# Self-attention on one core: residual on ScalarE, products and output bias on VectorE, reciprocal roots by a power on GpSimd

## The reference, cut to what matters

```python
# layer 0 (its attention part ends in this projection)
attn = softmax(logits) @ v            # 8 heads of 8
x = x + concat([conv_out, attn @ attn_w + attn_b])
# layer 1, self-attention, 1024 tokens of 256
u = (t - mean(t)) / sqrt(var(t) + 1e-5)
Q, K, V = u @ W_q, u @ W_k, u @ W_v   # 128 wide
out = softmax(Q @ K.T / sqrt(128)) @ V
t = t + out @ W_o + b_o + u           # u is added as well
v2 = (t - mean(t)) / sqrt(var(t) + 1e-5)   # input of the experts
```

## Time and profile before

| | |
|---|---|
| median of 3 runs | 2439.54 us (2436.12 to 2440.03) |
| profiled execution, its own time | 2439.41 us |
| its span | 2437.7 us |
| TensorE busy | 2185.6 us, 90% |
| VectorE busy | 1344.4 us, 55% |
| ScalarE busy | 1214.6 us, 50% |
| GpSimd busy | 330.2 us, 14% |
| mean granted TensorE clock | 0.929 |

### The profile page before, as it was taken

One profiled execution on the slowest core, in us unless ns is written; L12 is line 12 of the kernel. 1 busy time (PEld: TensorE's weight loads), 2 busy tenths in 40 slices (PEclk: granted clock), 3 DMA queues, 4 the chain that ended last, 5 costly groups with the idle time before them and its releaser, 6 DMA issues. The chain is left out here.

```text
span 2437.7 us, 32845 instructions
## 1 busy us (share of the span) xinstructions
PE 2185.6 (90%) x10534; PEld 1512.9 (62%) x10534; DVE 1344.4 (55%) x2054; ACT 1214.6 (50%) x2160; POOL 330.2 (14%) x274
## 2 busy tenths in 40 slices
PE   4999999947999999999999974988888893999997
PEld 3777888846445454444454422777777772888886
...
DMA packets 150472, 268.33 MB, mean 110 GB/s; under 512 B 31808, under 2 KB 94016, under 8 KB 146240
## 3 DMA queue, kind: packets, MB, share of 16 engines
...
...
...
## 5 line engine op out<-in xcount | busy, mean ns | idle before, releaser
L652 DVE TENSOR_REDUCE a_nmax<-a_sm 128x1 f32<-128x1024 f32 x512 | 604.0, 1220 | 209.9 <-PE a_sm L672 209.6
L908 ACT ACTIVATE p_shared<-a_st 128x512 f32<-128x512 f32 x1024 | 556.6, 596 | 252.4 <-PE a_st L933 250.9
L948 PE MATMUL a_pv<-p_shared,a_va 128*32 128x512 f32 x2048 | 275.1, 610 | 0.9 <-ACT p_shared L908 0.9
L933 PE MATMUL a_st<-a_qf,a_kf 121*128 121x512 f32 x704 | 257.5, 444 | 18.8 <-issue 8.6
L933 PEld LDWEIGHTS a_st<-a_qf,a_kf 121*128 121x128 f32 x704 | 121.0, 192 | 220.1 <-ACT p_shared L908 198.7
L672 PE MATMUL a_sm<-a_kf,a_qf 120*128 120x512 f32 x704 | 218.3, 429 | 40.8 <-DMA a_kf<-kq_d 25.0
L1823 PE MATMUL x_h_ps<-x_v_hi,x_w 128*128 128x512 f32 x512 | 181.0, 395 | 24.9 <-DVE x_v_lo L1764 24.9
L672 PEld LDWEIGHTS a_sm<-a_kf,a_qf 120*128 120x128 f32 x704 | 136.4, 204 | 78.8 <-issue 25.8
L1837 PE MATMUL x_y_ps<-x_h_hi,x_w 128*128 128x512 f32 x512 | 178.0, 389 | 0.0
L1774 DVE SCALAR_TENSOR_TENSOR x_h_lo<-x_hid,x_wts,x_h_hi 128x512 fp32r<-128x512 f32 x128 | 96.1, 751 | 138.3 <-ACT x_h_hi L1745 138.3
L1741 ACT ACTIVATE x_hid<-x_h_ps,x_b 128x512 f32<-128x512 f32 x128 | 88.4, 691 | 131.0 <-PE x_h_ps L1823 126.0
...
## 6 DMA issues: line engine op xcount, KB each, us to landing
...
```

The costliest lines, as they stand in the source:

```text
L652: nc.vector.tensor_reduce(nmax[:, h, t:t + 1], sm[k % 2][:], axis=AX.X, op=ALU.max, negate=True).then_inc(sm_read, 1)
L908: nc.scalar.activation(probs[:, t % 2, h, half * HALF:(half + 1) * HALF], st[half][:], ACT.Exp).then_inc(exp_done, 1)
L933: nc.tensor.matmul(st[half][:], kf[j][0:ROW_M + 1, h, t * P:(t + 1) * P], qf[j][0:ROW_M + 1, h, 2 * t // TT, half * HALF:(half + 1) * HALF ...
L948: m = nc.tensor.matmul(pv[32 * h:32 * h + 32, cols], va[j][:, t, h, :], probs[:, t % 2, h, cols], start=t == 0, stop=t == TT - 1, skip_gro ...
```

## The change

- `res` is a new step. On ScalarE it makes `xb` times (1 + rstd) plus `shift` in place, with four activations (t + u in one pass). VectorE makes `grow` = rstd + 1 in `apply`, and in `res` adds `bo` over 128x1024. `res 0` stands at the end of slot 5, `res 1` in slot 7, both at the end of `FRONT`.
- `norm` is a new step: the product of `att` and `rsb` on VectorE, in slots 0 and 1, at the head of `FRONT`. `proj 0` moves from slot 0 to slot 1.
- The reciprocal roots are one power (exponent -0.5) on GpSimd; the logarithms and exponentials on ScalarE and both uses of `newton` on VectorE go.
- ScalarE's `apply` no longer waits for `res_ready`.

```diff
         BETWEEN = [
-            [("out", 2, -1), ("probs", 7, -1), ("proj", 0, 1), ("vt", 1, 0), ("turn", 0, -1)],
-            [("probs", 0, 0), ("half", 3, -1), ("turn", 1, -1), ("mix", 0, 1)],
+            [("out", 2, -1), ("probs", 7, -1), ("norm", 0, 1), ("vt", 1, 0), ("turn", 0, -1)],
+            [("probs", 0, 0), ("proj", 0, 1), ("half", 3, -1), ("turn", 1, -1), ("norm", 1, 1), ("mix", 0, 1)],
...
-            [("turn", 3, -1), ("k", 0, 1), ("half", 1, 0), ("vt", 0, 1), ("apply", 1, 1)],
+            [("turn", 3, -1), ("k", 0, 1), ("half", 1, 0), ("vt", 0, 1), ("apply", 1, 1), ("res", 0, 1)],
...
-            [("q", 1, 1), ("probs", 6, 0), ("vvar", 0, 0), ("half", 2, 0), ("k", 1, 1), ("vapply", 0, 0), ("v", 1, 1), ("values", 2, 0)]]
+            [("q", 1, 1), ("probs", 6, 0), ("vvar", 0, 0), ("half", 2, 0), ("k", 1, 1), ("res", 1, 1), ("vapply", 0, 0), ("v", 1, 1),
+             ("values", 2, 0)]]
...
-                        if what == "proj":
...
-                            nc.gpsimd.tensor_tensor(att[k][:], att[k][:], rsb[k][:], ALU.mult).then_inc(norm_ready, 1)
-                        if what == "apply":
...
-                            nc.gpsimd.tensor_tensor(x1, x1, u[:], ALU.add)
...
-                            nc.gpsimd.tensor_tensor(x1, x1, bo_all, ALU.add).then_inc(res_ready, 1)
+                        if what == "var":
+                            pool.wait_ge(var_ready, n * 2 + k + 1)
+                            nc.gpsimd.tensor_tensor(rstd[:, k], var[:, k], power[:], ALU.pow).then_inc(rstd_ready, 1)
+                        if what == "vvar":
+                            pool.wait_ge(vart_ready, n * 2 + k + 1)
+                            nc.gpsimd.tensor_tensor(rstdt[:, k], vart[:, k], power[:], ALU.pow).then_inc(rstdt_ready, 1)
...
-                            act.wait_ge(res_ready, n * 2 + k + 1)
...
+                        elif what == "res":
+
+                            for i in range(QT):
+                                last = nc.scalar.activation(xb[s][:, k * QT + i, :], xb[s][:, k * QT + i, :], ACT.Identity,
+                                                            bias=shift[:, k, i:i + 1], scale=grow[:, k, i:i + 1])
+                            last.then_inc(grown_ready, 1)
...
+                            nc.vector.tensor_scalar(grow[:, k], rstd[:, k], 1.0, None, ALU.add)
+                            nc.vector.scalar_tensor_tensor(shift[:, k], mv[:, :, 0], -1.0, rstd[:, k], ALU.mult, ALU.mult).then_inc(shift_ready, 1)
+                        elif what == "res":
+                            dve.wait_ge(grown_ready, n * 2 + k + 1)
+                            x1 = xb[s][:, k * QT:(k + 1) * QT, :]
+                            nc.vector.tensor_tensor(x1, x1, bo_all, ALU.add).then_inc(res_ready, 1)
+                        elif what == "norm":
+
+                            dve.wait_ge(att_loaded[k], n * (16 * (1 + GROUPS)) + 16 * (1 + GROUPS))
+                            nc.vector.tensor_tensor(att[k][:], att[k][:], rsb[k][:], ALU.mult).then_inc(norm_ready, 1)
...
-                            newton(nc, dve, rstdt[:, k], vart[:, k], tmpt[:, k])
```

More of the change, by code:

```diff
@@ L999, in self_attention @@
         st6, mv = sb("b_st6", [P, QT, 6]), sb("b_mv", [P, QT, 2])
-        var, rstd, tmp, shift = (sb(f"b_{n}", [P, 2, QT]) for n in ("var", "rstd", "tmp", "shift"))
+        var, rstd, grow, shift = (sb(f"b_{n}", [P, 2, QT]) for n in ("var", "rstd", "grow", "shift"))
+        power = sb("b_power", [P, QT])
         u = sb("b_u", [P, QT, C])
@@ L1016, in self_attention @@
         st6t, mvt = sb("b_st6t", [P, QT, 6]), sb("b_mvt", [P, QT, 2])
-        vart, rstdt, tmpt = (sb(f"b_{n}", [P, 2, QT]) for n in ("vart", "rstdt", "tmpt"))
+        vart, rstdt = (sb(f"b_{n}", [P, 2, QT]) for n in ("vart", "rstdt"))
         v2 = sb("b_v2", [P, QT, C])
@@ L1031, in self_attention @@
         c_read = sem("b_c_read")
-        var_ready, rstd_ready, shift_ready, u_ready, res_ready = (sem(f"b_{n}_s") for n in ("var", "rstd", "shift", "u", "res"))
+        var_ready, rstd_ready, shift_ready, u_ready, grown_ready, res_ready = (
+            sem(f"b_{n}_s") for n in ("var", "rstd", "shift", "u", "grown", "res"))
         uhi_ready, bhi_ready = sem("b_uhi_s"), sem("b_bhi_s")
@@ L1063, in self_attention @@
              ("probs", 4, 0), ("turn", 2, -1), ("var", 1, 1), ("q", 0, 1), ("v", 0, 1)],
-            [("turn", 3, -1), ("k", 0, 1), ("half", 1, 0), ("vt", 0, 1), ("apply", 1, 1)],
+            [("turn", 3, -1), ("k", 0, 1), ("half", 1, 0), ("vt", 0, 1), ("apply", 1, 1), ("res", 0, 1)],
             [("out", 0, 0), ("values", 1, 0), ("ut", 2, 1), ("probs", 5, 0), ("out", 1, 0), ("ut", 3, 1)],
-            [("q", 1, 1), ("probs", 6, 0), ("vvar", 0, 0), ("half", 2, 0), ("k", 1, 1), ("vapply", 0, 0), ("v", 1, 1), ("values", 2, 0)]]
-        FRONT = [("proj", 0), ("proj", 1), ("mix", 0), ("mix", 1), ("mix", 2), ("var", 0), ("mix", 3), ("apply", 0), ("var", 1),
-                 ("ut", 0), ("ut", 1), ("apply", 1), ("sums", 0), ("q", 0), ("k", 0), ("v", 0), ("vt", 0), ("ut", 2), ("ut", 3), ("q", 1), ("k", 1), ("v", 1)]
+            [("q", 1, 1), ("probs", 6, 0), ("vvar", 0, 0), ("half", 2, 0), ("k", 1, 1), ("res", 1, 1), ("vapply", 0, 0), ("v", 1, 1),
+             ("values", 2, 0)]]
+        FRONT = [("norm", 0), ("norm", 1), ("proj", 0), ("proj", 1), ("mix", 0), ("mix", 1), ("mix", 2), ("var", 0), ("mix", 3), ("apply", 0), ("var", 1),
+                 ("ut", 0), ("ut", 1), ("apply", 1), ("sums", 0), ("q", 0), ("k", 0), ("v", 0), ("vt", 0), ("ut", 2), ("ut", 3), ("q", 1), ("k", 1), ("v", 1),
+                 ("res", 0), ("res", 1)]
         def period(b, s, before, after):
@@ L1205, in _ @@
             def _(pool):
+                nc.gpsimd.memset(power[:], -0.5)
                 nc.gpsimd.memset(wp[:], 0.0).then_inc(consts, 1)
@@ L1228, in _ @@
             def _(act):
-                def rsqrt(out, in_):
-                    nc.scalar.activation(out, in_, ACT.Ln)
-                    act.drain()
-                    return nc.scalar.activation(out, out, ACT.Exp, scale=-0.5)
                 def run(steps):
@@ L1251, in run @@
                                                  ).then_inc(b_read, 1)
-                        elif what == "var":
-                            act.wait_ge(var_ready, n * 2 + k + 1)
-                            rsqrt(rstd[:, k], var[:, k]).then_inc(rstd_ready, 1)
-                        elif what == "vvar":
-                            act.wait_ge(vart_ready, n * 2 + k + 1)
-                            rsqrt(rstdt[:, k], vart[:, k]).then_inc(rstdt_ready, 1)
                         elif what == "apply":
                             act.wait_ge(shift_ready, n * 2 + k + 1)
-                            act.wait_ge(res_ready, n * 2 + k + 1)
                             if k:
@@ L1318, in spread @@
                     nc.vector.tensor_scalar(v, m[:, :, 1], 1e-5, None, ALU.add).then_inc(ready, 1)
-                def scales(m, r, v, tm, sh, ready):
-                    newton(nc, dve, r, v, tm)
-                    nc.vector.scalar_tensor_tensor(sh, m[:, :, 0], -1.0, r, ALU.mult, ALU.mult).then_inc(ready, 1)
+                bo_all = bo[:].rearrange("p (a c) -> p a c", a=1).to_broadcast([P, QT, C])
                 def run(steps):
@@ L1366, in run @@
                             if k % 2 == 0:
-                                dve.wait_ge(res_ready, n * 2 + k // 2 + 2)
+                                dve.wait_ge(res_ready, n * 2 + k // 2 + 1)
                                 dve.wait_ge(t_stored[k // 2], n * 16 + 16)
@@ L1372, in run @@
                             last.then_inc(c_read, 1)
-                dve.sem_inc(res_ready, 1)
                 dve.wait_ge(sums_loaded[0], 16)
```

7 lines of the change are left out of this document (removed).

## The result

The changed kernel takes **2449.22 us** (median of 6 runs, 2446.65 to 2452.63) against 2439.61 us for the kernel before (6 runs, 2436.12 to 2440.37) on the same chip: +9.6 us, a ratio of 1.004 with a 95% interval of 1.0027 to 1.0052. The profiled execution took 2448.74 us with a span of 2447.0 and a mean granted clock of 0.937 (before 2439.41, 2437.7 and 0.929). So the change costs time, as forecast, but a third of the +27.1 us that the prediction added up. The steps that went as predicted and those that didn't are best seen apart, so the rows come first.

What follows compares the result with a forecast made beforehand. The prediction took TensorE, working in order almost without gaps, as busiest, with VectorE held by GpSimd in slot 4. Terms -31.2 + 26.6 + 12.2 + 5.6 + 7.9 + 6.5 - 0.5 = +27.1 gave 2466.5 us, range 2437 to 2482.

Steps and rivals of the forecast that it cites:

- the clock that stays up: Rival: the clock doesn't fall in the new TensorE gaps, so the change costs +9.4, 2449 us; chance 0.20.
- slot 4, images 1 to 6: Scores 4 to 5: without GpSimd's large operations holding VectorE, 5.2 us won per image, -31.2 us.
- slots 5 and 6, seven images, without clock: `res 0` delays the exponential of scores 6, and `out 1` waits: 3.8 us an image, +26.6 us.
- clock behind that gap: After TensorE's gap of some 3.6 us before `out 1` the clock falls in seven images, +12.2 us.
- slots 7, 0, 1: `res 1` delays the next scores 0 and `turn 0`, the projection moves to slot 1: 7 x 0.8, +5.6 us.
- two loop-backs: VectorE's 3.08 us of issue stays, TensorE's gap becomes 3.8 us and drops the clock: +7.9 us.
- front and image 0's slots 0, 1: Both `res` before the first exponential delay it 4.3 us, with clock and late `mixT`: +6.5 us.
- image 7 and the end, without slot 0: Image 7 has no next image and loses a `newton`: -0.5 us.
- 7 x 1.75: Price of the clock falling behind the gap before `out 1`, 1.75 us in each of seven images: +12.2 us.
- Powers: Roots on GpSimd, 1.67 us each, claimed hidden except in the front, their users coming 1.7 us or more later.
- The rule of the most loaded engine: Work on the busiest engine first: TensorE's work is unchanged, so time stays 2439.4 us; chance of no change 0.10.
- The rival of the hidden rest: Slot 4's held instructions go and the new waits mostly hide: 2420 us, chance 0.17.

Runs made afterwards that it cites:

- experiment 5: Changed kernel plus GpSimd's two 128x1024 additions again behind `u`, on a tile nobody reads or waits for: 2476.12 us.
- experiment 3: Changed kernel with `res 0` moved behind everything else of slot 6 on ScalarE and its bias addition into slot 7 on VectorE: 2416.57 us.
- experiment 8: Changed kernel with four extra VectorE drains in each `apply` and `vapply`, without small instructions: 2459.32 us.
- Experiment 10: Changed kernel with four small VectorE instructions into an unread tile and four drains in each `apply` and `vapply`: 2483.88 us.
- Experiment 2: Changed kernel with image 0's two residual passes moved out of the front into its own slots 1 to 3: 2443.87 us.
- Experiment 6: Kernel before with only the roots as powers on GpSimd, no `newton` or logarithm; products and additions stay on GpSimd: 2470.84 us.

## Why the prediction was wrong, and where it was right

It had the direction and the place, and the mechanism of the two largest terms, and the time is inside its range, but the amount was nearly three times too large. Two steps failed: the clock's price, given in full to every gap, and the gap of 3.8 us at the loop-backs, which never came. The result of 2449 is the value of one of the rivals, the clock that stays up. That is a coincidence: the clock fell in five of seven gaps, and what made up for it were the loop-backs and a larger gain in slot 4. By terms, predicted and measured (us):

| term | predicted | measured | |
|---|---|---|---|
| slot 4, images 1 to 6 | -31.2 | -35.3 | right, too small |
| slots 5 and 6, seven images, without clock | +26.6 | +25.3 (7 x 3.62) | right |
| clock behind that gap | +12.2 | about +6.7 | a fall in 5 of 7, mostly cheaper |
| slots 7, 0, 1 | +5.6 | about +7.5 | right, too small |
| two loop-backs | +7.9 | -1.1 | wrong |
| front and image 0's slots 0, 1 | +6.5 | +6.3 | right |
| image 7 and the end, without slot 0 | -0.5 | -1.7 | right, too small |
| image 0, slot 4 | 0 | +0.9 | not seen: `ut 1` waits 2.46 us there, not 1.81, and the clock falls |

The measured column adds up to +8.6 us; the phase also begins 0.6 later. Of the 18.5 us that the forecast had too much, the loop-backs are 9.0, the clock 5.5 and slot 4 4.1.

- **What goes.** GpSimd's operations held VectorE; experiment 5 puts them back without any dependence and 4.5 us of slot 4 return in each image (mean 14.92). The size was short because image 3's 16.03 us was taken for all, where the mean over images 1 to 6 is 16.26, and because a `turn` more was charged at 0.45 us, while the slot is 10.37 us with it. Of the 5.9 us won in each image, the wait gives 4.1 (5.65 to 1.58) and the clock and the rest 1.8, where the forecast had 3.2 and 2.0.
- **Slots 5 and 6.** The forecast had a gap of some 3.6 us ahead of `out 1`; it is 3.24 to 3.33 and slot 6 grew by 3.62 us where the clock stays up (10.49 beside 6.87), 3.8 being predicted. ScalarE's pass is 2.06 us, the addition 1.23, the maximum 1.22. That this placing is the cause is shown by experiment 3: without it 30 to 33 us are won.
- **The clock.** The step that failed is "7 x 1.75". The nearest rows gave no more than that 2.69 and 5.64 us had a fall and 1.81 had none, and one price was given to all seven. Measured: some 1.5 us in image 0, then 2.1, 1.1, 1.0 and 1.0 us in images 1, 2, 3 and 5, nothing in 4 and 6. With 3.62 us it falls in all six for 1.7 on average (experiment 8), and with 3.63 in all six for 1.0 to 1.1 (experiment 5). So 1.75 lies within what a fall cost, 1.0 to 2.1 us, at its upper side, and behind a gap of 3.3 us a fall may or may not come. A gap of 2.69 us with a fall and ones of 3.33 without show that length alone doesn't decide.
- **The loop-backs.** The step that failed is that the gap "becomes 0.69 + 1.93 + 1.2 = 3.8 us". It kept the 3.08 us of issue as if the loop had it whatever its body, while the change takes 64 instructions out of VectorE's loop body of two images (eight times `newton`, four small instructions and four drains each) and adds 12. The issue time fell to 0.61 and 0.55. Slots 0 and 1 together grew by 1.1 us at ordinary starts (12.06 beside 10.98) and by 0.56 and 0.53 at the loop-backs, so these two even win 1.1 us against the others. Experiment 10 restores the 3.08 and with it 4.4 us a loop-back: the pricing of the wait was about right, its condition was gone by the same edit.
- **The front.** First exponential late, a TensorE gap of 6.08 us ahead of the second scores, `mixT` late by 0.87: 8.14 - 4.10 + 7.71 - 4.20 = 7.55 us, less 1.3 won ahead of it, about as predicted. Experiment 2 gives 6.05 of it back.
- **Powers.** They are hidden in the changed kernel, as forecast, at 1.01 us each, but for 2.2 us in all that VectorE waits for two of them at image 7. Experiment 6 shows that this is no property of the power: with the products still on GpSimd they cost 8 us an image in slot 2 through the order of the queue.
- **The rule of the most loaded engine** (the Trainium skill, Perfetto Trace Analysis, section Identifying the Most-Contended Engine), taken alone as in the prediction, would have had no change. TensorE's work did stay (2185.6 and 2188.1 us busy), and yet kernels with the same 10534 matmuls, busy 2171.1 to 2198.8 us, lie between 2401.7 and 2483.9 us. Here it is the order of the short instructions on the engines behind TensorE that sets the time.

The rival of the hidden rest, put at 2420, needed the exponential of scores 6 to be less than 2 us late, and the edit put it 3.6 us late. With `res 0` elsewhere the time is 2416.57 us, near that rival's value.

**Open** are what the chip goes by when it lowers the clock after gaps of 3.3 us and whether the untraced executions fall in the same images, what in `newton`'s 64 instructions gives the loop-back its 3 us (their number, or instructions and drains side by side), why GpSimd holds `vapply`, and how much of experiment 6's slot 4 is the missing `newton` and how much its later start.
